# Scan, first chunk, attention side and x1 stage of a fused attention and FFN block

## The chip, the cores and the metric

The kernel runs on one core of one Trainium2 chip. The metric is device time in microseconds of one execution. "The span" is the time between the first and the last instruction that the profile of one execution shows.

## What is computed

1024 tokens of width 512 are normalised to `xn`. From it come two branches, and the output is `x + s * silu(f)`.

```python
xn = layernorm(x)
# attention-like branch: 4-bit weights, looked up in a table and scaled by blocks of 64, each with a rank-16 term
attn = (lin(xn, Wq) + lin(xn, Wk) + lin(xn, Wv)) / 3
x1 = xn + lin(attn, Wo)
h = silu(lin(x1, Wg)) * lin(x1, Wu)                  # 512 -> 1792
s = x1 + lin(h, Wd)                                  # 1792 -> 512
# FFN branch, weights from f32 pairs (w, mean)
W = mean + average(abs(w - mean)) * sign(w - mean)   # one average over a whole 1792x512 matrix, three matrices
f = lin(silu(lin(xn, W1)) * lin(xn, W3), W2)
out = x + s * silu(f)
```

## The kernel before

All products use f32r operands split in a high and a low part: three matmuls (high x high, high x low, low x high) per product. 1792 is cut in 14 chunks of 128; chunks 0 to 13 belong to the FFN branch, 14 to 27 to the second half of the 4-bit branch. A chunk's gate projection for one half of the tokens (512 columns) is 4 x 3 = 12 matmuls; so are its up projection and the other half. `h = silu(gate) * up` is made by ScalarE and VectorE and split. A down stage (D0 to D9) multiplies the `h` of two or three chunks with their down weights into 8 output tiles; three PSUM banks `down_ps` take turns, ScalarE evicts each (`y_evict`), and from D1 on GpSimd's queue adds the evicted tile to `y` or `y2` by an accumulating DMA (`y_add`, four slots `y_part`).

**Front.** The three averages need every element of `w - mean`. Chunks 0 to 3 are held on the chip as 12 units (gate 0 to 3, up 4 to 7, down 8 to 11; 128x512 pairs). Chunks 4 to 13 are only scanned: 15 tiles of 128x1024 pairs, 5 for each matrix, which go through a buffer of 4 slots (`scan`, L346). VectorE subtracts (L863), ScalarE writes the signs as int8 (L556), stores them to memory (L561) and sums the absolute values (L558). Units 0 to 3 are subtracted by VectorE, 4 to 11 by GpSimd (L506), and summed by ScalarE (L574). `take_coeff(m)` reduces the partial sums (L906), TensorE adds them over the partitions (`total`, L1235), VectorE scales them (L909). Then a unit is made (`unit_make`, L916), its high part is written by ScalarE (L584) and its low part by VectorE (L924), and TensorE projects. All gate projections of chunks 0 to 3 come first, then all up projections, then D0. `total(UP)` stands on TensorE's queue behind `project(3, GATE, 0)`, `total(DOWN)` behind `project(2, UP, 1)`.

**Middle.** From D0 on the order is written out in `STAGES`: D0, 4, 5, 6, D1, 7, 8, 9, D2, 10, 11, 12, D3, 13, X, D4, T, 14 and so on. A numbered stage (`phase`) projects that chunk. Each engine goes through the stages in this order. VectorE makes the weights of the next FFN chunk from `base` and the stored `sign` (`ffn_make`, L932), both loaded by SP (`load_ffn`). Beside this runs the attention side: the product of Wo with the sum of Wq, Wk and Wv is folded to one 512x512 matrix `MT`. It takes 40 steps (`attn_step`: a ramp on ScalarE, L668, and a min-add on VectorE, L1002; five steps for half a row block, codes by `load_attn`), some more for sums and splits, and 24 small groups of matmuls into the one bank `side_ps` (`ATTN_SIDE` lists behind which projection or tile each stands: per row block of 4, `lora_qkv`, `lora_o` and four `fold`s, L1303). Each needs the bank emptied by VectorE (L1015, L1019, L1032), the folds also the low parts (L1023, L1025). `ATTN_COUNT` lists the steps per stage.

**x1, D4, T.** Stage X computes x1 = MT times xn in 8 tiles (L1356), which replace xn in `xT` (high ScalarE L822, low VectorE L1182). D4 is the last down stage of the FFN branch, T the rank-16 part of gate and up (L1369, high L831, low L1195). In between run the first steps for the 4-bit chunks (`nf4_step`, ramp L688, VectorE L1041, scale L1047, and the rank term `lora_add` L948). On GpSimd's queue: `y_add` for D1 to D3, then four additions that sum the parts of x1 to `y2` (L524), then `y_add` for D4. On SP's queue, in this order around D2: ..., load_attn(5), a wait for the end of D2, A_down (L436), load_ffn(11), load_ffn(12), load_attn(6), load_ffn(13), load_attn(7), ...; `B_gu` (the rank terms' second factor) is loaded in two halves into one buffer (L448, L453), scaled (L742), split (L749, L1108), and the first use of its gate half and of T is the 13th matmul of a projection of chunk 14 (L1258).

## Time and profile before

| | |
|---|---|
| time of 3 runs, us | 665.79 (662.33 to 666.79) |
| the profiled execution, us | 665.82 |
| its span, us | 664.0 |
| TensorE matmul busy | 558.6 us, 84% |
| VectorE busy | 463.6 us, 70% |
| ScalarE busy | 376.4 us, 57% |
| GpSimd busy | 113.3 us, 17% |
| moved by DMA | 76.72 MB |

The profile is of one execution. "Busy" is the time in which an engine executes; the shares are averages over stages of very different kinds, so they are to be read stage by stage. The granted clock is TensorE's, as a share of 2.4 GHz. A row of idle time names what ended it.

### The profile page before, as it was taken

The page shows a single profiled execution, that of the slowest core. Times are in us where ns is not written, and L with a number is a line of the kernel's source. Part 1 is how long each engine was busy: PE and PEld are TensorE (multiplying, and loading weights), DVE is VectorE, ACT ScalarE, POOL GpSimd, SP SyncE. Part 2 cuts the span into 40 slices and gives each one's busy share as a digit, 9 for nine tenths or more (in the row PEclk, how much of TensorE's full clock was granted, in tenths as well). Part 3 has the DMA queues.
Part 4 walks back from the last instruction along what each step waited for, and adds up shares of the span by engine and source line. Part 5 has one row for each costly group of instructions (what it writes and reads, how often), then busy time and mean ns, then how long its engine had stood idle before and what let it go on. Part 6 is the DMA issues. An engine that isn't in the chain of part 4 may idle for free.

```text
span 664.0 us, 6488 instructions
## 1 busy us (share of the span) xinstructions
PE 558.6 (84%) x2304; PEld 447.9 (67%) x2304; DVE 463.6 (70%) x512; ACT 376.4 (57%) x494; POOL 113.3 (17%) x110
## 2 busy tenths in 40 slices
PE   1168688999999759888698479989899998999997
PEld 1155466888888647667586257767677886887886
DVE  6770548688887628772419947888888888988436
ACT  3866576657744634542237265587559667676310
POOL 0021323001300310022000930012004002101491
PEclk9778888999999888998988778979999999999999
DMA  9979531131820472045201362247217325623903
GB/s 339 401 272 391 209 117 63 61 126 41 178 84 0 80 216 84 0 105 107 52 1 33 74 122 60 61 91 155 59 33 138 80 57 122 123 59 80 221 1 126
DMA packets 37951, 76.72 MB, mean 116 GB/s; under 512 B 3872, under 2 KB 11936, under 8 KB 37920
## 3 DMA queue, kind: packets, MB, share of 16 engines
q1 hardware_dynamic: 24624, 57.57, 27.4%
q0 software_dynamic: 9216, 16.78, 14.2%
q10 hardware_dynamic: 4080, 1.97, 1.0%
q8 instruction: 18, 0.29, 0.2%
q14 instruction: 13, 0.11, 0.1%
HBM read 55.46 MB, written 4.06 MB: 90 GB/s over the span
## 4 chain that ended last, share of the span: by engine, by line
PE 45%; DVE 23%; ACT 14%; issue 10%; DMA 4%; POOL 2%; SPq 0%; ACTq 0%; DVEq 0%
PE down_ps L1278 17%; PE up_ps L1250 13%; PE gate_ps L1250 10%; DVE acc L1041 9%; ACT ramp L688 5%; POOL y L524 2%; PE side_ps L1303 2%; ACT sign_st L556 2%; PE down_ps L1356 2%; DVE up_ps L958 1%; DVE scan L863 1%; DMA sign<-sign_kept 1%; DMA scan<-in_mean 1%; ACT y_part L635 1%; DMA y<-y_part 1%
## 5 line engine op out<-in xcount | busy, mean ns | idle before, releaser
L1278 PE MATMUL down_ps<-h,dn 128*128 128x512 f32 x672 | 169.7, 410 | 18.9 <-ACT y_part L635 18.9
L1250 PE MATMUL up_ps<-xT,gu 128*128 128x512 f32 x672 | 167.4, 401 | 11.2 <-DVE h L963 11.1
L1250 PE MATMUL gate_ps<-xT,gu 128*128 128x512 f32 x672 | 168.0, 402 | 10.3 <-ACT silu_gate L617 7.2
L1278 PEld LDWEIGHTS down_ps<-h,dn 128*128 128x128 f32 x672 | 132.4, 199 | 52.2 <-ACT y_part L635 23.4
L1250 PEld LDWEIGHTS up_ps<-xT,gu 128*128 128x128 f32 x672 | 130.6, 195 | 41.6 <-issue 9.7
L1250 PEld LDWEIGHTS gate_ps<-xT,gu 128*128 128x128 f32 x672 | 129.8, 194 | 41.2 <-issue 9.3
L1041 DVE SCALAR_TENSOR_TENSOR acc<-ramp,acc 128x1536 f32<-128x1536 f32 x56 | 102.4, 1829 | 30.4 <-ACT ramp L688 29.7
L514 POOL DMA_DIRECT2D y<-y_part x64 | 55.5, 933 | 383.3 <-ACT y_part L635 383.2
L688 ACT ACTIVATE ramp<-codes,ramp_bias 128x1536 f32<-128x1536 uint8 x70 | 109.8, 1574 | 1.2 <-DVE acc L1041 1.2
L622 ACT ACTIVATE h<-up_ps 128x512 fp32r<-128x512 f32 x56 | 33.5, 597 | 112.7 <-DVE up_ps L955 60.0
L635 ACT ACTIVATE y_part<-down_ps 128x512 f32<-128x512 f32 x64 | 37.5, 596 | 45.5 <-PE down_ps L1278 33.1
L1002 DVE SCALAR_TENSOR_TENSOR attn_acc<-attn_ramp,attn_acc 128x1024 f32<-128x1024 f32 x40 | 49.4, 1235 | 14.7 <-ACT attn_ramp L668 14.6
L963 DVE TENSOR_TENSOR h<-up_ps,h 128x512 fp32r<-128x512 f32 x56 | 38.5, 688 | 16.6 <-ACT h L622 16.4
L617 ACT ACTIVATE silu_gate<-gate_ps 128x512 f32<-128x512 f32 x56 | 32.9, 587 | 22.9 <-PE gate_ps L1250 12.7
L668 ACT ACTIVATE attn_ramp<-attn_codes,ramp_bias 128x1024 f32<-128x1024 uint8 x40 | 45.8, 1144 | 0.0
L1041 DVE SCALAR_TENSOR_TENSOR acc<-ramp,codes 128x1536 f32<-128x1536 f32 x14 | 24.5, 1752 | 15.2 <-ACT ramp L688 15.1
L1303 PE MATMUL side_ps<-w_o,w_qkv 128*128 128x512 f32 x48 | 15.5, 434 | 22.1 <-DVE MT_acc L1032 15.5
L932 DVE SCALAR_TENSOR_TENSOR base<-sign,coeff,base 128x512 f32<-128x512 int8 x30 | 23.7, 844 | 12.9 <-DMA sign<-sign_kept 12.9
L955 DVE TENSOR_TENSOR up_ps<-silu_gate,up_ps 128x512 f32<-128x512 f32 x28 | 19.4, 692 | 17.5 <-PE up_ps L1250 17.5
L958 DVE SCALAR_TENSOR_TENSOR up_ps<-up_ps,silu_gate 128x512 f32<-128x512 f32 x28 | 19.4, 694 | 12.8 <-PE up_ps L1258 12.8
L1303 PEld LDWEIGHTS side_ps<-w_o,w_qkv 128*128 128x128 f32 x48 | 9.1, 201 | 26.4 <-issue 17.0
L1047 DVE SCALAR_TENSOR_TENSOR acc<-acc,scale 128x1536 f32<-128x1536 f32 x14 | 24.6, 1758 | 0.5
(155 smaller groups left out, 508.0 us busy)
## 6 DMA issues: line engine op xcount, KB each, us to landing
y<-y_part POOLq DMA_DIRECT2D x64, 256.0 KB, 3.6
...
scan<-in_w SPq DMA_DIRECT2D x15, 512.0 KB, 7.4
scan<-in_mean SPq DMA_DIRECT2D x15, 512.0 KB, 8.3
...
```

What stands on the lines that cost most here:

```text
L514: pool.dma_start((y if g < FFN_GROUPS else y2)[:, hq, sl], y_part[:, q % Y_SLOTS, :], accum_op=ALU.add).then_inc(y_added[q % Y_SLOTS], 16)
L617: nc.scalar.activation(silu_buf(k, th), gate_ps[th][:, :], ACT.Silu, scale=1.0 if k < B0 else UNIT_STEP).then_inc(silu_done, 1)
L622: nc.scalar.activation(h_part(k, HI, th), up_ps[th][:, :], ACT.Copy).then_inc(h_hi, 1)
L635: nc.scalar.activation(place, down_ps[n % 3][:, :], ACT.Copy, scale=1.0 if g < FFN_GROUPS else UNIT_STEP).then_inc(y_out, 1)
L668: nc.scalar.activation(attn_ramp[:, s % 2, :, :], attn_codes[:, a % 2, :, :], ACT.Relu, bias=ramp_bias[:, 0, j:j + 1], scale=slope).then_i ...
L688: nc.scalar.activation(ramp[:, s % 2, :], codes[:, k % 2, :], ACT.Relu, bias=ramp_bias[:, 1, j:j + 1], scale=slope).then_inc(nf4_ramped, 1)
L963: nc.vector.tensor_tensor(h_part(k, LO, th), up_ps[th][:, :], h_part(k, HI, th).bitcast(f32), ALU.subtract).then_inc(h_lo, 1)
L1002: nc.vector.scalar_tensor_tensor(attn_acc[:, a % 2, :, :], attn_ramp[:, s % 2, :, :], NF4_RAMPS[j][2], attn_acc[:, a % 2, :, :], ALU.min, ...
L1041: nc.vector.scalar_tensor_tensor(acc[k % 2][:, :], ramp[:, s % 2, :], UNIT_RAMPS[j][2], codes[:, k % 2, :] if j == 0 else acc[k % 2][:, :] ...
L1250: last = nc.tensor.matmul(ps[:, :], w[:, w_part, hc * P:(hc + 1) * P], xT[:, x_part, hc, th * HALF:(th + 1) * HALF], start=(hc == 0 and w_ ...
L1278: last = nc.tensor.matmul(down_ps[n % 3][:, :], dn[:, k % DN_SLOTS, w_part, hq * P:(hq + 1) * P], h_part(k, h_p, th), start=(k == ks[0] an ...
L1303: last = nc.tensor.matmul(side_ps[:, :], w_qkv[:, a_part, hc * P:(hc + 1) * P], w_o[:, b_part, :], start=(a_part == b_part == HI), stop=(a ...
```

## The change

1. *Scan.* The buffer becomes two: 5 slots for w and 3 for mean; mean is loaded first, and its slot is free when the subtraction is done, w's when sign and sum are. 4 slots for signs instead of 2. Subtractions of tiles 7, 9, 11 and 13 move from VectorE to GpSimd, the absolute sums of tiles 3, 4, 6, 8, 9, 11, 13 and 14 from ScalarE to VectorE (`tensor_reduce`).
2. *First chunk.* The gate projection of chunk 0 is computed as mean part (24 matmuls, `early_mean`) plus coefficient times sign part (16 matmuls, `early_signs`; signs need no low part), which VectorE adds (`early_sum`). Unit 0 is never made. Chunks 1 and 3 use `gate_ps` for their up projection, so that the wait for `h_lo` is for two chunks back. The orders of ScalarE and VectorE are rewritten.
3. *Attention side.* New `ATTN_COUNT` and `ATTN_SIDE`; MT's high and low parts are made inside stage 13; loads of SP are reordered.
4. *x1, D4, T.* Two 4-bit steps come ahead of x1's evictions; `y2` is filled by a DMA of the high part (SP) and four accumulating DMAs of the low part (GpSimd's queue), behind D4's `y_add`; T's parts come before the step of that stage; in down stages of two chunks the steps stand behind tiles 0, 3, 5, 7.

```diff
-SCAN_SLOTS = 4
-SIGN_SLOTS = 2
+SCAN_W, SCAN_MEAN = 5, 3
+SIGN_SLOTS = 4
+POOL_SCAN = [7, 9, 11, 13]
+DVE_SUMS = [3, 4, 6, 8, 9, 11, 13, 14]
...
-ATTN_COUNT = {"D0": (0, 3), 4: (0, 3), 5: (0, 2), 6: (0, 4), "D1": (0, 4), 7: (0, 3), 8: (0, 2), 9: (0, 4),
-              "D2": (0, 4), 10: (0, 3), 11: (0, 2), 12: (0, 4), "D3": (0, 8), 13: (0, 5)}
+ATTN_COUNT = {"D0": (0, 3), 4: (0, 3), 5: (0, 2), 6: (0, 4), "D1": (0, 4), 7: (0, 3), 8: (0, 3), 9: (0, 5),
+              "D2": (0, 4), 10: (0, 3), 11: (0, 3), 12: (0, 4), "D3": (0, 7), 13: (3, 0)}
...
-ATTN_SIDE = [(4, 3), ("D1", 0), (7, 0), (7, 2), (8, 0), (8, 2),
-             (8, 3), (9, 2), ("D2", 2), ("D2", 5), ("D2", 7), (10, 1),
-             (10, 2), (11, 0), (12, 2), ("D3", 0), ("D3", 1), ("D3", 3),
-             ("D3", 4), ("D3", 5), (13, 0), (13, 1), (13, 2), (13, 3)]
+ATTN_SIDE = [(4, 3), ("D1", 0), (7, 0), (7, 2), (7, 3), (8, 1),
+             (8, 2), (8, 3), ("D2", 1), ("D2", 3), ("D2", 5), ("D2", 7),
+             (10, 0), (10, 1), (11, 3), (12, 1), (12, 2), ("D3", 0),
+             ("D3", 1), ("D3", 3), ("D3", 6), ("D3", 7), (13, 0), (13, 1)]
...
             def load_scan(k):
...
-                if k >= SCAN_SLOTS:
-                    sp.wait_ge(scan_abs, k - SCAN_SLOTS + 1)
+                if k >= SCAN_MEAN:
+                    diff_wait(sp, k - SCAN_MEAN)
+                sp.dma_start(scan_mean[:, k % SCAN_MEAN, :].rearrange("p (c n) -> p c n", c=2),
...
+                if k >= SCAN_W:
+                    sp.wait_ge(scan_sign, k - SCAN_W + 1)
+                    sum_wait(sp, k - SCAN_W)
+                sp.dma_start(scan_w[:, k % SCAN_W, :].rearrange("p (c n) -> p c n", c=2),
...
             load_attn(5)
+            load_ffn(11)
+            load_attn(6)
+            load_ffn(12)
             sp.wait_ge(down_done, 3 * TT)
             sp.dma_start(A_down_raw[0:ROWS3, 0:INTER], A_down_in).then_inc(A_down_loaded, 16)
-            load_ffn(11)
-            load_ffn(12)
-            load_attn(6)
+            load_attn(7)
             load_ffn(13)
-            load_attn(7)
...
-            load_scale(B0 + 1)
-            load_codes(B0 + 2)
+            sp.wait_ge(x1_lo, TT)
+            sp.wait_ge(MT_lo, HC)
+            sp.dma_start(y2[:, :, :], xT[:, HI, :, :].bitcast(f32)).then_inc(y2_copied, 16)
             sp.wait_ge(B_gu_hi, 1)
             sp.wait_ge(B_gu_lo, 1)
             sp.dma_start(B_gu_raw[0:ROWS3, 0:INTER], B_gu_in[:, UP, :]).then_inc(B_gu_loaded, 16)
+            load_scale(B0 + 1)
+            load_codes(B0 + 2)
...
-            for u in range(FIRST, UNITS):
-                unit_subtract(u)
+            for kind in (UP, DOWN):
+                for n in range(SCAN_TILES):
+                    if scan_on_pool(SCAN_TILES * kind + n):
+                        scan_subtract(SCAN_TILES * kind + n)
+                    if n > 0:
+                        unit_subtract(FIRST * kind + n - 1)
             attn_tables()
-            for g in range(1, FFN_GROUPS - 1):
+            for g in range(1, FFN_GROUPS):
                 y_add(g)
-            pool.wait_ge(x1_lo, TT)
+            pool.wait_ge(y2_copied, 16)
             for hc in range(HC):
-                nc.gpsimd.tensor_tensor(y2[:, hc, :], xT[:, HI, hc, :].bitcast(f32), xT[:, LO, hc, :].bitcast(f32),
-                                        ALU.add).then_inc(y2_ready, 1)
-            y_add(FFN_GROUPS - 1)
-            pool.wait_ge(y2_ready, HC)
+                pool.dma_start(y2[:, hc, :], xT[:, LO, hc, :].bitcast(f32), accum_op=ALU.add).then_inc(y2_ready, 16)
+            pool.wait_ge(y2_ready, 16 * HC)
...
+            def early_high():
+                act.wait_ge(unit_loaded[0], 32)
+                nc.scalar.activation(gu_weight(0, GATE)[:, HI, :], unit_base(0), ACT.Copy).then_inc(gu_hi, 1)
+
+            def early_sign():
+                act.wait_ge(unit_diff_dve, 1)
+                nc.scalar.activation(sign_T, unit_raw(0), ACT.Sign).then_inc(unit_sign, 1)
...
+            def scan_sum(k):
+                kind, n = k // SCAN_TILES, k % SCAN_TILES
+                diff_wait(dve, k)
+                nc.vector.tensor_reduce(abs_sums[:, SUMS * kind + n:SUMS * kind + n + 1], scan_w[:, k % SCAN_W, :],
+                                        axis=AX.X, op=ALU.add, apply_absolute_value=True).then_inc(scan_abs_dve, 1)
...
+            def early_sum(th):
+                dve.wait_ge(gate_done, th + 1)
+                nc.vector.tensor_scalar(silu_buf(0, th), up_ps[th][:, :], coeff[:, GATE:GATE + 1], None, ALU.mult
+                                        ).then_inc(early_part, 1)
+                dve.wait_ge(early_part, th + 1)
+                nc.vector.tensor_tensor(early_ps[th][:, :], early_ps[th][:, :], silu_buf(0, th), ALU.add
+                                        ).then_inc(early_gate, 1)
...
+            early_mean(0)
+            early_mean(1)
+            early_signs(0)
             total(GATE)
-            for c in range(FIRST):
+            early_signs(1)
+            for c in range(1, FIRST):
```

VectorE's new order in the front (sums moved to it are bold): x_low 0 to 3, early_low, unit_subtract(0), x_low 4 to 7, subtract 2, unit 1, subtract 3, unit 2, **sum 3**, subtract 4, unit 3, **sum 4**, take_coeff(GATE), unit_make(1), early_sum(0), unit_low(1), subtract 5, unit_make(2), early_sum(1), unit_low(2), unit_make(3), subtract 6, unit_low(3), **sum 6**, subtract 8, **sum 8**, **sum 9**, take_coeff(UP), unit_make 4, 5, low 4, make 6, low 5, make 7, low 6, subtract 10, low 7, **sum 11**, h_make(0, 0), subtract 12, h_low(0, 0), h_make(0, 1), h_low(0, 1), **sum 13**, h_make(1, 0), subtract 14, h_low(1, 0), **sum 14**, h_make(1, 1), h_low(1, 1), take_coeff(DOWN).

## Rows read from the trace of the kernel before

**Rows 1.** The page of the profile, its first line.

```profile
span 664.0 us, 6488 instructions
```

**Rows 2.** Busy time by stage: window, length, engines, granted clock, DMA share, GB/s.

```profile
38.40:109.60 71.20, 55.23 (x197) 42.60 (x198) 37.48 (x49) 44.40 (x82) 15.34 (x14) 0.86 0.61 216
109.60:217.80 108.20, 108.20 (x478) 89.25 (x476) 88.75 (x106) 67.85 (x92) 13.62 (x13) 1.00 0.28 75
217.80:331.70 113.90, 87.81 (x353) 69.84 (x352) 64.81 (x84) 47.77 (x66) 13.25 (x16) 0.91 0.39 94
331.70:399.20 67.50, 50.30 (x183) 38.71 (x184) 43.17 (x31) 34.68 (x39) 20.62 (x12) 0.82 0.28 56
399.20:660.20 261.00, 251.13 (x1064) 201.84 (x1062) 201.83 (x183) 158.60 (x177) 48.40 (x48) 0.98 0.41 91
```

**Rows 3.** Timeline of TensorE, front: start us, us, engine, line, count, idle before.

```profile
38.40 7.32 PE L1250 MATMUL gate_ps<-xT,gu 128*128 128x512 f32 x24 [2.73 <-DVE gu L924]
...
73.84 5.61 PE L1250 MATMUL up_ps<-xT,gu 128*128 128x512 f32 x24
...
109.48 16.48 PE L1278 MATMUL down_ps<-h,dn 128*128 128x512 f32 x72
```

**Rows 4.** Timeline of ScalarE, front: an Abs and the issue of a store.

```profile
28.80 1.04 ACT L558 ACTIVATE scan<-scan 128x1024 f32<-128x1024 f32 x1
28.92 0.37 ACTq L561 DMA_DIRECT2D sign_kept<-sign_st  x1
```

**Rows 5.** Timeline of VectorE, front: subtraction, partial sum, coefficients, last low parts.

```profile
23.39 0.68 DVE L899 TENSOR_TENSOR xT<-side_ps,xT 128x512 fp32r<-128x512 f32 x1
...
27.45 1.23 DVE L863 TENSOR_TENSOR scan<-scan 128x1024 f32<-128x1024 f32 x1
...
34.80 0.16 DVE L906 TENSOR_REDUCE abs_part<-abs_sums 128x1 f32<-128x9 f32 x1 [5.53 <-ACT junk L574]
...
66.62 0.16 DVE L909 TENSOR_SCALAR coeff<-side_ps 128x1 f32<-128x1 f32 x1 [7.17 <-PE side_ps L1235]
...
98.60 0.16 DVE L909 TENSOR_SCALAR coeff<-side_ps 128x1 f32<-128x1 f32 x1 [3.21 <-PE side_ps L1235]
...
104.70 1.28 DVE L924 TENSOR_TENSOR dn<-unit_lr,dn 128x512 fp32r<-128x512 f32 x2
```

**Rows 6.** GpSimd's subtractions of unit_lr: min/median/max ns.

```profile
L506 POOL TENSOR_TENSOR unit_lr<-unit_lr x2: 1277/2358/3439, 65.9 to 69.7; 128x512 f32<-128x512 f32 x2
```

**Rows 7.** DMA of the first 75 us in 40 slices, and an issue's time to landing.

```profile
GB/s 3 322 375 364 371 409 402 406 406 398 405 404 398 405 403 401 399 398 404 399 401 400 189 0 74 196 383 373 365 398 406 403 382 400 409 405 84 0 0 70
...
scan<-in_mean SPq DMA_DIRECT2D x15, 512.0 KB, 8.3
```

**Rows 8.** Who waited for whom, 200 to 420 us: total, times, longest.

```profile
PE side_ps L1303 <- DVE MT_acc L1032: 15.5, 4, 9.4
DVE base L932 <- DMA sign<-sign_kept: 12.9, 1, 12.9
...
PE side_ps L1303 <- DVE w_o L1025: 6.7, 3, 3.7
...
PE down_ps L1356 <- DVE MT L1204: 4.0, 1, 4.0
```

**Rows 9.** Timeline of SP's queue: the load of sign for chunk 11.

```profile
236.11 0.42 SPq L365 DMA_DIRECT2D sign<-sign_kept  x1
```

**Rows 10.** Who waited for whom, 200 to 420 us: TensorE in D4.

```profile
PE down_ps L1278 <- ACT y_part L635: 11.9, 2, 9.5
```

**Rows 11.** Timeline of GpSimd: the sum of x1's parts.

```profile
366.29 13.68 POOL L524 TENSOR_TENSOR y<-xT 128x1024 f32<-128x1024 f32 x4 [52.87 <-DVE xT L1182]
```

**Rows 12.** Timeline of VectorE and ScalarE: B_gu's low part and high part.

```profile
363.46 2.02 DVE L1108 TENSOR_TENSOR B_gu<-B_gu_raw,B_gu 32x1792 fp32r<-32x1792 f32 x1
...
332.28 1.70 ACT L749 ACTIVATE B_gu<-B_gu_raw 96x1792 fp32r<-96x1792 f32 x1
```

**Rows 13.** DMA queues, 360 to 400 us: packets, MB, share of 16 engines.

```profile
q0 software_dynamic: 1152, 2.10, 29.2%
```

More of the change, by code:

```diff
@@ L1117, in _ @@
                 x_low(t)
+            early_low()
             unit_subtract(0)
@@ L1200, in _ @@
                         A_down_low()
-                    if stage == 13:
-                        for c in range(HC):
-                            dve.wait_ge(MT_hi, c + 1)
-                            nc.vector.tensor_tensor(MT[:, LO, c, :], MT_acc[:, c, :], MT[:, HI, c, :].bitcast(f32),
-                                                    ALU.subtract).then_inc(MT_lo, 1)
                 else:
```

279 lines of the change are left out of this document (195 added, 84 removed).

## Prediction

> **What bounds the kernel now.** I read the busy time by stages first, because shares of the whole span mix stages with different limits. The span is 664.0 us [rows 1]. From 109.6 to 217.8 us TensorE is busy the whole 108.20 us with 478 matmuls at granted clock 1.00: 108.20/478 = 0.226 us per matmul of 512 columns. That is the pace of a stage with nothing to gain. With it the other stages can be priced: time lost = length minus matmuls x 0.226. From 38.4 to 109.6: 71.2 - 197 x 0.226 = 26.7 us lost. From 217.8 to 331.7: 113.9 - 353 x 0.226 = 34.1. From 331.7 to 399.2: 67.5 - 183 x 0.226 = 26.1. From 399.2 to 660.2: 261.0 - 1064 x 0.226 = 20.5 [rows 2]. With the 38.4 us before the first projection these are all that can be won; TensorE's own work is the bound everywhere else. A part of each loss is the clock: it is 0.86, 0.91 and 0.82 in the first three of these stages, so a pause is paid twice, by itself and by matmuls at 1.2 instead of 2.4 GHz after it.
>
> **Front: scan, first chunk.** Before, TensorE starts its projections at 38.40, the up projections at 73.84 and D0 at 109.48 [rows 3]. What it waits for are three coefficients on VectorE: the first partial sum comes at 34.80 and its coefficient 0.9 later, the other two coefficients at 66.62 and 98.60 [rows 5]. Each comes after the last of the absolute sums. ScalarE pays for a tile an Abs of 1.04 and a sign of the same shape [rows 4], some 2.1 us.
>
> *Gate coefficient.* Tiles 3 and 4 now have their sums on VectorE. A reduction of 128x1024 isn't in the trace. Nearest: the subtraction of the same shape, 1.23 us [rows 5]; bounds 0.68 (half the width, the x_low row) and 2.46 (twice the subtraction); I take 1.15. ScalarE does not save a full Abs: the store of the signs waits for the sign and then takes 0.37 on its queue, which the Abs used to cover [rows 4]; so a tile without Abs costs about 1.5, saving 0.65, not 1.1. ScalarE also gets early_high and early_sign (0.5 each). Stepping through the two orders from the last x_low (start 23.39, moved 0.6 later by early_low): VectorE does subtract 2, unit 1, subtract 3, unit 2, sum 3, subtract 4, unit 3, sum 4, ending at 32.2; ScalarE ends its fourth unit sum at 31.8. The partial sum comes at 32.2 instead of 34.80, the coefficient at 33.1.
>
> *First chunk.* early_mean is 24 matmuls in place of the 24 of chunk 0, early_signs 16 more (16 x 0.226 = 3.6 us of extra TensorE work). 32 of these run from 21.7 to about 30.7, in today's pause, and hide. The last 8 come while VectorE makes unit 1. Chunk 1 starts at about 36.6, with chunk 0 done: as if the old 38.40 were 31.2 (36.6 less 24 x 0.226). The added vector work is early_sum (2 x 1.3) and early_low (0.6), that taken away one unit_make.
>
> *Up coefficient.* Here is the big term. Before, TensorE reached total(UP) only after project(3, GATE, 0), which waited for a silu that stood behind full scan tiles on ScalarE. Now the scan of tiles 5 to 9 has three Abs less and two subtractions on GpSimd. I step SP too: the mean buffer has 3 slots and is freed by the subtraction, so tiles 5 to 9 are issued at about 26, 28, 30, 37 and 42 us. The data flow at 400 GB/s when the queue is full, and a tile lands 8.3 us after issue in such a queue [rows 7]; tile 9 lands at 47. GpSimd's subtraction of 128x1024 isn't in the trace; half the width takes 1.28 alone and 3.44 at worst beside VectorE [rows 6], so 2.6 to 6.9; I take 2.6 with 1 us of waiting. Then tile 9's difference is there at 49 to 50, its sum at 51, the last unit sum at 51.3, the coefficient at 52.5. Up projections start at 56 to 57 instead of 73.84.
>
> *Down coefficient.* The load now bounds it. x, 15 tile pairs of 1.05 MB and 12 unit pairs of 0.52 MB are 24.1 MB, 60 us at 400 GB/s; 3 us start, some 3 for the stored signs and 4 to 6 of pauses (mean 13 waits for subtraction 10, which follows the up coefficient's unit work) make 70 to 72. Behind it stand subtraction 14, sum 14, two h steps and the total: coefficient at about 77 to 79 instead of 98.60. TensorE pauses 2 to 4 us at total(DOWN). From coefficient to the third unit's low part it took 98.60 to 105.98 = 7.4 us [rows 5]; I keep 7.4, so D0 starts at 86.5 (82 to 92) instead of 109.48. **Term 1: -23 us** (-17 to -27).
>
> On GpSimd the Trainium skill (SBUF — State Buffer, "Who interferes with whom") says that a VectorE instruction with two SBUF inputs contends with a GpSimd instruction that reads SBUF, and that one blocks the other whole, while tensor_reduce never contends. The trace's 3.44 against 1.28 us agrees with the first half [rows 6]. By that rule up to 4 x 2.6 = 10.4 us of VectorE work would be pushed back, and term 1 could shrink to about -15.
>
> **Attention side, 217.8 to 331.7.** TensorE pauses before the fold matmuls for 15.5 us (4 times, longest 9.4) behind MT_acc and 6.7 us (3 times) behind w_o, and 4.0 before the x1 stage behind MT's low part [rows 8]; with the slow clock after each that is the stage's 34.1.
>
> The 9.4: VectorE sat 12.9 us for sign of chunk 11 [rows 8], whose load was issued at 236.11, right behind A_down's, which waits for the end of D2 [rows 9]. Moving load_ffn(11), load_attn(6) and load_ffn(12) ahead of that wait frees it: load_ffn(11) needs only chunk 9's split. A_down, load_attn(7) and load_ffn(13) then follow at D2's end and are needed in stage 11 or later, one stage of 48 matmuls (10.9 us) away, against at most 8.3 us of landing [rows 7]. Worth 9.4 + 1.6 of clock = 11.
>
> The rest: attention steps come 1 to 2 steps earlier from stage 8 on and the folds sit later relative to them: a fold of the second row block follows its low parts by a stage part, and the last four sit at D3 6, 7 and 13 0, 1 with MT's splits inside stage 13 in place of behind it. That removes the 6.7, the other 6.1 and the 4.0, with about 6 us of clock: 23. Against it stands VectorE. Over 109.6 to 217.8 it was busy 88.75 of 108.20 with 25 attention steps and, beside them, two down stages and six phases [rows 2]. Stages 7 to 12 (D2 among them) now hold 25 steps, six phases and one down stage in 91 us of TensorE time (400 matmuls): 88.75 less some 5 for the down stage's own work is 84, or 92%, and stage 9 alone has five steps where four were the most. So I expect short waits of 4 to 5 us in all. **Term 2: -29 us** (-17 to -33).
>
> **x1, D4 and T, 331.7 to 399.2.** GpSimd's y2 sum takes 13.68 us ahead of D4's additions [rows 11]; TensorE waits 9.5 us behind y_part because of it, and 2.4 more there [rows 10]. Now D4's additions go first; y2 is filled by a DMA and four accumulating DMAs, needed only in D5. By stepping: VectorE ends x1's low part 3 only 0.5 earlier (the steps still lie between), but lora_add comes some 4 us earlier, since one step and the scaling no longer stand ahead and GpSimd's reads no longer run beside it; with the 9.5 and 2.4 gone and some 3 of slow clock, D4 ends about 14 us earlier, at 371 to 373. Then B_gu's second half is late next: its load is behind the 2.1 MB copy on SP's queue. The nearest price is the accumulating queue, 2.10 MB in 29.2% of 40 us = 11.7 us [rows 13]; D4's own additions are as much again at the same time. So copy and additions fill 361 to about 380, B_gu lands at 378 to 382, its scaling and high part (1.70 each) and its low part (2.02) [rows 12] end at 386, and T's low part at 386 to 387; TensorE stands some 7 us at the first matmul with T. That point was 399.2, the end of the stage [rows 2]. **Term 3: -13 us** (-2 to -18). load_scale(15) and load_codes(16), now behind B_gu, are wanted only after T: nothing.
>
> **Late part.** D5's steps are spread over its short tiles; of the 20.5 us lost there [rows 2] I take 3 (0 to 6). **Term 4: -3.**
>
> **Sum.** 664.0 - 23 - 29 - 13 - 3 = 596.0 us of span. The profiled execution took 665.82 us, 1.8 over its span and equal to the median of 665.79: **597.8, say 598 us**.
>
> **Rivals.** (a) *GpSimd holds back the scan*: its subtractions take up to 6.9 us and block VectorE; tiles 7, 9 and 13 each cost 3 to 4 more on the path: term 1 becomes -13, 608 us. For it: 3.44 us; against: sums on VectorE have one input. 14 in 100. (b) *The copy delays B_gu by its full price*: if D4's additions, the copy and the accumulations run one after another at the accumulating queue's rate, 3 x 11.7 = 35 us from 361, then B_gu's 2 + 5.4, T comes at 403 and term 3 is +4: 615 us. 10 in 100. (c) *VectorE becomes the bound of the attention side*, stages 9 to 12 run 8 to 12 us over: 609 us. 12 in 100. (d) *It goes better*: no residual waits, B_gu in time: 583 or less. 8 in 100. (e) *Slower than before*: denser matmuls are held at 1.2 GHz. Each costs 0.226 more; to eat 68 us, 301 more than now would have to run so, one in eight. Against it the 478 matmuls in a row at clock 1.00 [rows 2]. 2 in 100. The forecast itself, 585 to 606 with its terms' errors, has 54.
>
> The range 583 to 612 takes in (a), (c) and the forecast. About 1% is what a measurement can tell from no change. Faster by over 1% (under 659) is every case but (e): 97 in 100; same 1; slower 2.
>
> **What would show it.** D0's first matmul at about 86; coefficients at 33, 52 and 78; tensor_reduce near 1.15 us and GpSimd's subtraction near 2.6; no load of sign waiting on VectorE's path at D2; no pause over 2 us before folds; D4 over by 373 and a pause of about 7 us before the first T matmul. The forecast is wrong if D0 starts after 95, if VectorE's waits turn into TensorE's in stages 9 to 12, or if B_gu lands after 390.

## The result and the profile after

The changed kernel takes 614.35 us (median of 4 runs, 612.87 to 614.86), the kernel before in the same comparison 666.29 us (4 runs, 662.33 to 667.77). The ratio is 0.9225, 95% interval 0.9182 to 0.9269: 7.7% faster. Predicted were 598 us and a range of 583 to 612. The sign was right; the gain was 52 us where 68 were forecast, and the time lies 2.4 us above the range. One execution of the kernel before (830.77 us) and one of a kernel below (779.53 us) showed a granted clock near 0.66, and no figure here uses them.

The profiled execution has a span of 612.2 us. Cut at the same four points as the sum of the prediction (gate projections, D0, x1, first matmul behind T), the stages are the following. Columns as in [rows 2]: window, length, busy us and count of TensorE, its weight loads, VectorE, ScalarE, GpSimd, then granted clock, DMA share and GB/s.

```profile
36.35:91.20 54.85, 45.74 (x174) 35.69 (x173) 44.95 (x50) 36.03 (x65) 25.14 (x19) 0.87 0.82 293
91.20:285.99 194.79, 189.20 (x830) 154.69 (x828) 154.24 (x191) 117.32 (x161) 27.49 (x28) 1.00 0.41 102
285.99:345.96 59.97, 46.17 (x184) 35.76 (x184) 32.44 (x30) 33.29 (x38) 10.45 (x12) 0.90 0.51 116
345.96:608.40 262.44, 251.36 (x1064) 202.61 (x1062) 204.93 (x183) 158.91 (x178) 48.38 (x48) 0.98 0.42 95
```

The boundaries of the kernel before are 109.48 [rows 3], 331.68 and 399.22 in its timeline (331.70 and 399.20 in [rows 2]), and 660.2 us. So the terms measured are:

| term | before | after | measured | predicted |
|---|---|---|---|---|
| 1: up to D0 | 109.48 | 91.20 | -18.3 | -23 (-17 to -27) |
| 2: D0 to x1 | 222.20 | 194.79 | -27.4 | -29 (-17 to -33) |
| 3: x1 to behind T | 67.54 | 59.97 | -7.6 | -13 (-2 to -18) |
| 4: late part | 261.0 | 262.4 | +1.5 | -3 (0 to -6) |
| sum of the span | 664.0 | 612.2 | -51.8 | -68 |

All four terms fell short, by 4.7, 1.6, 5.4 and 4.5 us. Three of them are within their own bounds; the fourth is outside, and all four missed in one direction. The second row shows what term 2 brought: 194.79 us for the stretch in which 188 us of matmuls at full speed stand (830 at 0.226), at a clock of 1.00 where it was 0.95 before over the same stretch. The profiles of six kernels of this study that leave this stretch as it is have 196.5 to 196.6 us here and not 194.8, so term 2 is -25.7 to -27.4 us.

**Front after.** VectorE's timeline (start us, us, engine, line, operation, shapes, count, idle time before it and what ended it):

```profile
33.37 0.16 DVE L1012 TENSOR_SCALAR coeff<-side_ps 128x1 f32<-128x1 f32 x1 [0.48 <-PE side_ps L1391]
...
40.45 2.47 DVE L1027 TENSOR_TENSOR gu<-unit_st,gu 128x512 fp32r<-128x512 f32 x1
42.84 1.77 DVE L1019 SCALAR_TENSOR_TENSOR unit_st<-unit_st,coeff 128x512 f32<-128x512 f32 x1
44.54 1.21 DVE L960 TENSOR_TENSOR scan_w<-scan_w,scan_mean 128x1024 f32<-128x1024 f32 x1
...
53.47 1.22 DVE L966 TENSOR_REDUCE abs_sums<-scan_w 128x1 f32<-128x1024 f32 x1 [2.52 <-POOL scan_w L572]
...
56.40 0.16 DVE L1012 TENSOR_SCALAR coeff<-side_ps 128x1 f32<-128x1 f32 x1 [0.68 <-PE side_ps L1391]
...
66.54 1.21 DVE L960 TENSOR_TENSOR scan_w<-scan_w,scan_mean 128x1024 f32<-128x1024 f32 x1
...
73.12 0.69 DVE L1058 TENSOR_TENSOR up_ps<-silu_gate,up_ps 128x512 f32<-128x512 f32 x1
...
83.44 0.16 DVE L1012 TENSOR_SCALAR coeff<-side_ps 128x1 f32<-128x1 f32 x1 [0.68 <-PE side_ps L1391]
```

and GpSimd's of the same time:

```profile
39.97 2.40 POOL L572 TENSOR_TENSOR scan_w<-scan_w,scan_mean 128x1024 f32<-128x1024 f32 x1 [1.38 <-DMA scan_w<-in_w]
42.32 1.75 POOL L567 TENSOR_TENSOR unit_st<-unit_st 128x512 f32<-128x512 f32 x1
...
51.07 2.36 POOL L572 TENSOR_TENSOR scan_w<-scan_w,scan_mean 128x1024 f32<-128x1024 f32 x1 [4.18 <-DMA scan_w<-in_w]
53.41 1.26 POOL L567 TENSOR_TENSOR unit_st<-unit_st 128x512 f32<-128x512 f32 x1
...
73.07 2.41 POOL L572 TENSOR_TENSOR scan_w<-scan_w,scan_mean 128x1024 f32<-128x1024 f32 x1 [7.00 <-DMA scan_w<-in_w]
```

Two unit instructions of VectorE, which take 0.68 and 0.75 us elsewhere in the same view, take 2.47 and 1.77 here. Each ends 0.5 us after a GpSimd subtraction does: 40.45 + 2.47 = 42.92, and GpSimd's ends at 42.37; 42.84 + 1.77 = 44.61, and GpSimd's at 44.07. Five more such rows stand between 37 and 66 us, of 1.76 to 2.43 us, and each of them ends 0.5 to 0.6 us behind GpSimd's too. Two kinds of VectorE's instructions run beside GpSimd without being stretched: the reduction at 53.47 has its usual 1.22 us beside GpSimd's instruction of 53.41, and the h step at 73.12, one of whose inputs lies in PSUM, takes 0.69 beside that of 73.07. The three coefficients come at 33.37, 56.40 and 83.44, against 35.7, 66.62 and 98.60 before (the first is the 34.80 of [rows 5] and 0.9).

**x1, D4 and T after.** Who waited for whom, 286 to 348 us (total us, times, longest), and then the DMA issues of 290 to 380 us (count, KB of one, median us from issue to landing):

```profile
ACT y_part L716 <- DMA y<-y_part: 12.5, 4, 5.3
...
PE gate_ps L1420 <- DVE T L1337: 7.3, 1, 7.3
...
PE down_ps L1440 <- ACT y_part L716: 4.0, 2, 3.8
```

```profile
y<-y_part POOLq DMA_DIRECT2D x8, 256.0 KB, 11.2
y<-xT SPq DMA_DIRECT2D x1, 2048.0 KB, 11.0
y<-xT POOLq DMA_DIRECT2D x4, 512.0 KB, 8.8
B_gu_raw<-in_B_gu SPq DMA_DIRECT2D x1, 672.0 KB, 15.8
```

TensorE's 9.5 us wait of [rows 10] has become 3.8. ScalarE stands 12.5 us for y_part's slots, as long as in the kernel before, from 331.7 to 400 us:

```profile
ACT y_part L635 <- DMA y<-y_part: 12.4, 3, 10.2
```

Then GpSimd's sum held the additions back, which landed 4.9 us after their issue; now they are issued in time and take 11.2 us to land.

### The profile page after: what moved, and what is told of

It reads as the page before. It is cut to its first block, busy times and chain, and to the rows that moved or that the text cites. A ratio compares the mean times of both kernels' runs of the same rounds, so it can differ in the third digit from the quotient of the medians.

```text
span 612.2 us, 6544 instructions
## 1 busy us (share of the span) xinstructions
PE 549.9 (90%) x2320; PEld 442.9 (72%) x2320; DVE 467.6 (76%) x519; ACT 367.3 (60%) x478; POOL 112.3 (18%) x114
## 4 chain that ended last, share of the span: by engine, by line
PE 40%; DVE 25%; issue 13%; ACT 11%; DMA 7%; SPq 1%; POOL 1%; ACTq 0%; DVEq 0%
PE down_ps L1440 13%; PE up_ps L1412 10%; PE gate_ps L1412 10%; DVE acc L1144 9%; ACT ramp L769 7%; DMA y<-y_part 4%; DMA scan_w<-in_w 2%; DVE up_ps L1061 2%; PE side_ps L1465 2%; DVE scan_w L960 2%; DVE h L1066 1%; PE down_ps L1518 1%; DVE attn_acc L1105 1%; ACT y_part L716 1%; DMA unit_end<-in_mean 1%
## 5 line engine op out<-in xcount | busy, mean ns | idle before, releaser
L1412 PE MATMUL gate_ps<-xT,gu 128*128 128x512 f32 x696 | 174.3, 404 | 1.2 <-ACT silu_gate L698 0.5
L1440 PE MATMUL down_ps<-h,dn 128*128 128x512 f32 x672 | 161.2, 395 | 11.3 <-ACT y_part L716 11.3
L1412 PEld LDWEIGHTS gate_ps<-xT,gu 128*128 128x128 f32 x696 | 136.0, 196 | 32.5 <-DVE gu L1027 1.5
L1440 PEld LDWEIGHTS down_ps<-h,dn 128*128 128x128 f32 x672 | 126.5, 190 | 42.3 <-ACT y_part L716 14.8
L1412 PE MATMUL up_ps<-xT,gu 128*128 128x512 f32 x624 | 152.0, 395 | 4.4 <-DVE h L1066 3.8
L1412 PEld LDWEIGHTS up_ps<-xT,gu 128*128 128x128 f32 x624 | 118.6, 191 | 31.4 <-DVE h L1066 4.5
L1144 DVE SCALAR_TENSOR_TENSOR acc<-ramp,acc 128x1536 f32<-128x1536 f32 x56 | 98.3, 1756 | 43.0 <-ACT ramp L769 42.4
L703 ACT ACTIVATE h<-up_ps 128x512 fp32r<-128x512 f32 x52 | 31.1, 598 | 100.7 <-DVE up_ps L1061 51.8
L1066 DVE TENSOR_TENSOR h<-up_ps,h 128x512 fp32r<-128x512 f32 x52 | 35.7, 686 | 15.2 <-ACT h L703 15.1
L698 ACT ACTIVATE silu_gate<-gate_ps 128x512 f32<-128x512 f32 x54 | 31.7, 588 | 23.0 <-PE gate_ps L1412 15.8
L1058 DVE TENSOR_TENSOR up_ps<-silu_gate,up_ps 128x512 f32<-128x512 f32 x24 | 16.6, 691 | 11.8 <-PE up_ps L1412 11.8
L1040 DVE TENSOR_TENSOR gu<-acc,gu 128x1024 fp32r<-128x1024 f32 x14 | 17.0, 1217 | 5.5 <-ACT gu L675 5.5
L1135 DVE TENSOR_TENSOR MT_acc<-MT_acc,side_ps 128x512 f32<-128x512 f32 x16 | 10.9, 681 | 12.7 <-PE side_ps L1465 12.7
```

What stands on the lines that cost most here:

```text
L698: nc.scalar.activation(silu_buf(k, th), ps[:, :], ACT.Silu, scale=1.0 if k < B0 else UNIT_STEP).then_inc(silu_done, 1)
L703: nc.scalar.activation(h_part(k, HI, th), up_bank(k, th)[:, :], ACT.Copy).then_inc(h_hi, 1)
L1066: nc.vector.tensor_tensor(h_part(k, LO, th), up_bank(k, th)[:, :], h_part(k, HI, th).bitcast(f32), ALU.subtract).then_inc(h_lo, 1)
L1144: nc.vector.scalar_tensor_tensor(acc[k % 2][:, :], ramp[:, s % 2, :], UNIT_RAMPS[j][2], codes[:, k % 2, :] if j == 0 else acc[k % 2][:, :] ...
L1412: last = nc.tensor.matmul(ps[:, :], w[:, w_part, hc * P:(hc + 1) * P], xT[:, x_part, hc, th * HALF:(th + 1) * HALF], start=(hc == 0 and w_ ...
L1440: last = nc.tensor.matmul(down_ps[n % 3][:, :], dn[:, k % DN_SLOTS, w_part, hq * P:(hq + 1) * P], h_part(k, h_p, th), start=(k == ks[0] an ...
```

## The experiments

Each kernel is the changed kernel with the edit shown. Ratios are to the kernel before on the same chip, with their 95% intervals; for the changed kernel itself it is 0.9225 [0.9182, 0.9269] and 614.35 us. Intervals overlap where kernels differ by 3 us or less, so such differences are read from boundaries in the profiles too.

### Front: GpSimd's subtractions

```
-POOL_SCAN = [7, 9, 11, 13]
+POOL_SCAN = []
```

> The changed kernel with tiles 7, 9, 11 and 13 of the scan subtracted by VectorE again (everything else of the change stays). Theory (GpSimd's reads slow VectorE's instructions with two SBUF inputs, and so cost the front about as much as they save): the instructions of unit_make and unit_low between 37 and 47 us and between 59 and 67 us fall from 1.8 and 2.4 us to about 0.75 and 0.7 where only a tile subtraction lay beside them; VectorE does 4 x 1.15 us more; D0 starts at 88 to 92 instead of 91.2, the whole within 0.5% of the changed kernel (609 to 617). Rival (the offload is a plain gain, the loss lies elsewhere): D0 4 to 5 us later, 617 to 620.

Measured: 611.71 us, 0.9203 [0.917, 0.9236]. VectorE's timeline:

```profile
33.25 0.16 DVE L1012 TENSOR_SCALAR coeff<-side_ps 128x1 f32<-128x1 f32 x1 [0.68 <-PE side_ps L1391]
...
40.32 0.68 DVE L1027 TENSOR_TENSOR gu<-unit_st,gu 128x512 fp32r<-128x512 f32 x1
...
54.30 0.16 DVE L1012 TENSOR_SCALAR coeff<-side_ps 128x1 f32<-128x1 f32 x1 [0.48 <-PE side_ps L1391]
...
78.58 0.16 DVE L1012 TENSOR_SCALAR coeff<-side_ps 128x1 f32<-128x1 f32 x1 [0.48 <-PE side_ps L1391]
```

The low part at 40 us is back at 0.68, and the coefficients are 2.1 and 4.9 us earlier, although VectorE does four subtractions more. Its groups of instructions by line, 34 to 90 us, give the account. The subtractions cost 14.0 us for ten instead of 7.3 for six: 6.7 us had been moved to GpSimd. The seven low parts of line L1027 and the eight products of unit_st, line L1019, cost 5.9 + 7.0 us instead of 10.5 + 9.1: 6.7 us had come back as blocking. What is left of blocking in this kernel (1.78 us at 37 and at 60 us, 2.32 at 41) stands beside the unit subtractions, which GpSimd made before the change as well. So the move took nothing off VectorE, while a difference made by GpSimd takes 2.4 us and not 1.2, and VectorE waited 2.52 us for that of tile 9 (the row at 53.47 above). D0 starts at 86.02 instead of 91.20, and at 87.41 in a later kernel with the same front. The prediction had said 86.5, but for a kernel in which GpSimd does subtract.

Only about half of that arrives at the end (2.6 us of the medians):

```profile
86.02:284.23 198.21, 192.58 (x829) 157.12 (x829) 154.63 (x191) 117.41 (x161) 27.49 (x28) 0.98 0.41 101
```

The stretch from D0 to x1 is 198.21 us instead of 194.79 with the same 4.8 us of waits for folds; the granted clock is 0.98 instead of 1.00. D0's 72 matmuls take 18.25 us behind a pause of 1.89, instead of 16.48 without one (granted clock 0.91 instead of 1.00), and 12 matmuls behind the fold pause at 243 us take 4.12 instead of 2.90 (0.67 over 243.6 to 248.7, where the changed kernel has 1.00). So 1.2 GHz was granted for a part of each. The second of these isn't the edit's: behind the same pause of 2.8 us the clock stayed at 1.00 in four profiles of this study and fell in six others that leave this stretch as it is. With the late copy (below) the same edit moves D0 from 90.95 to 87.41 and x1 from 287.43 to 284.01, and the median by 3.7 us, so there it arrives in full.

### Front: one more slot for the means

```
-SCAN_W, SCAN_MEAN = 5, 3
+SCAN_W, SCAN_MEAN = 4, 4
```

> The changed kernel with 4 slots for w and 4 for mean instead of 5 and 3 (the same memory). Theory (the loads of tiles 9 and 13 are late because the mean slot is freed by a subtraction of three tiles back, which stands behind coefficient work on VectorE): tile 9 is issued at about 40 instead of 45.8, tile 13 at 55 to 58 instead of 67.8, coefficients at 52 to 54 and 76 to 79, D0 at 84 to 87 instead of 91.2, so 607 to 610. Rival (the data rate bounds the front, 24 MB at 400 GB/s): issues earlier, landings the same, D0 within 1 us, 613 to 615.

Measured: 612.43 us, 0.9217 [0.9183, 0.9252]; coefficients at 33.68, 55.67, 82.52, D0 at 89.96. The mean of tile 9 is issued at 38.64 instead of 45.78 and that of tile 13 at 55.22 instead of 67.77, that is 7 and 12.5 us earlier. The coefficients moved by 0.7 and 0.9. So the issue of the loads was not what held them; 1.9 us of time can't be told from nothing.

### Front: subtraction 10 ahead of the up coefficient

```
             scan_sum(9)
+            scan_subtract(10)
             take_coeff(UP)
...
             unit_low(6)
-            scan_subtract(10)
             unit_low(7)
```

> The subtraction of scan tile 10 goes ahead of the up coefficient on VectorE; before, it stood behind that coefficient's unit work and ended at 67.8 us. Theory (down coefficient late because mean 13 waits for subtraction 10): mean 13 is issued 8 to 11 us earlier, at 57 to 60; the down coefficient comes at 77 to 80 instead of 83.4, D0 at 85 to 88 instead of 91.2; the up coefficient 1.2 to 2.4 us later (57.6 to 59). Of the 4 to 5 us, 1 to 4 reach the end: 611 to 613. Rival (the stored signs, the units and the total amount of data bound it): the down coefficient stays within 1.5 us of 83.4, time 614 to 616.

Measured: 614.75 us, 0.9223 [0.9179, 0.9266]: the rival. VectorE's two coefficients:

```profile
58.36 0.16 DVE L1012 TENSOR_SCALAR coeff<-side_ps 128x1 f32<-128x1 f32 x1 [0.68 <-PE side_ps L1391]
...
83.83 0.16 DVE L1012 TENSOR_SCALAR coeff<-side_ps 128x1 f32<-128x1 f32 x1 [0.56 <-PE side_ps L1391]
```

The mean of tile 13 is issued at 57.64 instead of 67.77, 10 us earlier, as the theory had it, and the down coefficient still comes at 83.83. My theory of what delays it fell. Put side by side over the kernels of this study, the distance from the up to the down coefficient is 83.44 - 56.40 = 27.0 us in the changed kernel, 24.3 without GpSimd's part, 26.9 with four mean slots, 25.5 here and, in the three kernels with both cures below, 24.2, 25.7 and 26.2. The two shortest issued tile 13's mean at 57.48 and 63.10, the kernel with 26.9 at 55.22 and the one with 26.2 at 53.73, so the distance doesn't follow the loads. It does scatter: 24.3 and 25.7 are of the same front, and six kernels with the changed kernel's front have 26.2 to 27.1. The rows between the two coefficients show VectorE working through its fixed order, with a wait of only 0.34 us for a load: low parts, subtractions and sums in between, and each h step behind the up projections, which start behind the up coefficient; the last sum (79.48 to 80.69 in the changed kernel) is followed by two h steps of chunk 1, and then comes the total. That the order is the bound is read from these rows. No kernel changed the order of the h steps, so it is not shown.

### Attention side: the order of the loads

```
-            load_ffn(11)
-            load_attn(6)
-            load_ffn(12)
             sp.wait_ge(down_done, 3 * TT)
             sp.dma_start(A_down_raw[0:ROWS3, 0:INTER], A_down_in)...
+            load_ffn(11)
+            load_attn(6)
+            load_ffn(12)
```

> Only the order of SyncE's loads is undone: A_down's load with its wait for the end of D2 stands again ahead of chunk 11's codes and signs, attention step 6 and chunk 12. Theory (term 2: 11 of the 29 us came from here): the time returns to 614.4 + 11 = about 625 us (622 to 628), VectorE waits some 9 to 12 us for the sign of chunk 11 during D2, and TensorE stands 7 to 9 us in one piece before a fold in stage 11 or 12. Rival (the moved steps and folds alone bring the 27 us and VectorE had slack): the wait on VectorE returns but TensorE loses under 3 us: 614 to 617.

Measured: 624.28 us, 0.9366 [0.9324, 0.9408], 9.9 us slower. TensorE's timeline and who waited for whom, 190 to 300 us:

```profile
226.12 0.79 PE L1452 MATMUL side_ps<-A_qkv,B_qkv_hi 128*128 128x512 f32 x1 [8.37 <-DVE MT_acc L1135]
```

```profile
ACT attn_acc L743 <- DMA attn_codes<-in_codes_attn: 13.9, 1, 13.9
```

The pause of 8.37 us is back, and x1 comes 297.15 - 90.52 = 206.6 us after D0 instead of 194.8: 11.8 us in this stretch, or 10.1 against the 196.5 of most kernels. The size is that of the step. The one who waits for a late load is ScalarE, for the codes of an attention step, and no longer VectorE for the sign of chunk 11 as in [rows 8].

### Attention side: steps, folds and MT's splits

```
-              ... 8: (0, 3), 9: (0, 5),
-              ... 11: (0, 3), 12: (0, 4), "D3": (0, 7), 13: (3, 0)}
+              ... 8: (0, 2), 9: (0, 4),
+              ... 11: (0, 2), 12: (0, 4), "D3": (0, 8), 13: (0, 5)}
 ATTN_SIDE = [... the list of the kernel before ...]
 MT_high(), MT_low(c): behind phase(13), as before
```

> The tables of attention steps and folds are those of the kernel before, and the splits of MT follow stage 13 as they did; the new order of SyncE's loads stays. Theory (term 2 in two parts: 10 us from the loads, as their undoing showed with 624.3 us, the rest of the 27.4 from steps and folds): 614.4 + 15 to 18 = 629 to 632 us; TensorE waits behind MT_acc and w_o before folds and some 4 us before the x1 stage. Rival (with the load no longer late, VectorE catches up by itself and the old folds cost little): 617 to 622.

Measured: 630.21 us, 0.9457 [0.9418, 0.9496], 15.9 us slower. TensorE's timeline, the longest pauses:

```profile
203.13 1.65 PE L1460 MATMUL side_ps<-w_o,w_qkv 128*128 128x512 f32 x3 [3.70 <-DVE w_o L1127]
...
272.16 1.62 PE L1460 MATMUL side_ps<-w_o,w_qkv 128*128 128x512 f32 x3 [3.57 <-DVE MT_acc L1134]
...
303.69 10.12 PE L1513 MATMUL down_ps<-xT,MT 128*128 128x512 f32 x36 [3.19 <-DVE MT L1198]
```

The waits behind w_o (6.7 us, 3 times, as in [rows 8]), three behind MT_acc and one behind MT return; x1 comes 212.7 us after D0, 17.9 more. With the 11.8 of the loads this is 29.7, and both together had brought 27.4. Both kernels run slow behind a fold pause of 2.8 and 2.6 us, as those with 196.5 do; against these the halves are 10.1 and 16.2, together 26.3, where term 2 is -25.7. The two halves of term 2 are shown and add up: 11 predicted for the loads, 18 for steps and folds.

### x1 to T: the copy to y2, later

```
-            sp.wait_ge(x1_lo, TT)
-            sp.wait_ge(MT_lo, HC)
-            sp.dma_start(y2[:, :, :], xT[:, HI, :, :].bitcast(f32)).then_inc(y2_copied, 16)
             sp.wait_ge(B_gu_hi, 1)
...
             load_codes(B0 + 2)
+            sp.wait_ge(x1_lo, TT)
+            sp.wait_ge(MT_lo, HC)
+            sp.wait_ge(y_out, TT * FFN_GROUPS)
+            sp.dma_start(y2[:, :, :], xT[:, HI, :, :].bitcast(f32)).then_inc(y2_copied, 16)
```

> The changed kernel with the copy of x1's high part to y2 moved on SP's queue behind B_gu's second half, scale and codes, and held back until D4's tiles are evicted. Theory (copy and D4's additions share the DMA engines, so additions land in 11.2 us instead of 3.6 and B_gu in 15.8 instead of 5): additions land in under 5 us, ScalarE's waits for y_part (12.5 us) and TensorE's (3.8 us) go, B_gu lands at about 322, the wait of 7.3 us for T falls under 1 us; with slow clock 12 to 15 us less: 600 to 603. Rival (ScalarE and VectorE's steps bound this stretch, the waits only lie in their slack): the same stretch is at most 4 us shorter: 610 to 613.

Measured: 607.23 us, 0.9137 [0.9098, 0.9175], 7.1 us less than the changed kernel. DMA issues, 290 to 380 us, and TensorE's first matmul with T:

```profile
y<-y_part POOLq DMA_DIRECT2D x8, 256.0 KB, 8.6
...
B_gu_raw<-in_B_gu SPq DMA_DIRECT2D x1, 672.0 KB, 5.5
```

```profile
338.93 0.79 PE L1421 MATMUL gate_ps<-T,B_gu 96*128 96x512 f32 x1 [2.65 <-DVE T L1338]
```

From x1 to this matmul it is 338.93 - 287.43 = 51.5 us, in the changed kernel 345.37 - 285.99 = 59.4. So the copy at its old place cost 7.9 us there, and nearly all of it reaches the end. The 12 to 15 us that I expected were too much: the additions still take 8.6 us to land.

### x1 to T: B_gu ahead of the copy

```
             sp.wait_ge(B_gu_hi, 1)
             sp.wait_ge(B_gu_lo, 1)
             sp.dma_start(B_gu_raw[0:ROWS3, 0:INTER], B_gu_in[:, UP, :]).then_inc(B_gu_loaded, 16)
+            (the copy to y2 and its two waits, moved here)
```

> The copy to y2 goes behind the load of B_gu's second half on SyncE's queue, and so still runs beside D4's additions; before, it went ahead of it. Theory (two separate costs: B_gu late behind the copy, and D4's additions slowed beside it; only the first goes): B_gu lands in 5 to 8 us, but the additions stay at 9 to 11 us, TensorE's waits in D4 stay at 2 to 4 us and T waits 4 to 7 us, because ScalarE, which scales B_gu, stands behind y_part's slots: 611 to 614 us. Rival (B_gu's late landing is the whole of the missing 5.5 us): as with the copy behind D4, 607 to 608.

Measured: 613.1 us, 0.9196 [0.9158, 0.9234]: no difference that can be told. DMA issues, then ScalarE's and TensorE's timelines:

```profile
y<-y_part POOLq DMA_DIRECT2D x8, 256.0 KB, 10.1
...
B_gu_raw<-in_B_gu SPq DMA_DIRECT2D x1, 672.0 KB, 5.6
```

```profile
333.43 0.60 ACT L716 ACTIVATE y_part<-down_ps 128x512 f32<-128x512 f32 x1 [7.57 <-DMA y<-y_part]
...
340.24 1.68 ACT L834 ACTIVATE B_gu_raw<-B_gu_raw 96x1792 f32<-96x1792 f32 x1
```

B_gu's half lands 5.6 us after its issue at 318.31, by 324, and ScalarE scales it only at 340.24, because it stood 7.57 us for a slot of y_part. TensorE waits 10.4 us at T. From x1 to the first T matmul it is 56.55 us, against 57.8 to 59.9 in the seven kernels with both the copy and B_gu at the changed kernel's places and 51.3 to 51.5 in those with the late copy. This tells the two causes apart: B_gu's late landing, which the prediction named, is worth 1 to 3 us at most of the 8; what decides is that D4's additions land late beside the copy, and that the in-order ScalarE has B_gu behind them. When TensorE ends D4 doesn't decide either: here, with four mean slots and with the old pace of D5 it ended 37.6 to 37.9 us after x1, 5 us earlier than in the changed kernel, and then waited 10.4, 12.2 and 11.7 us at T.

### x1 to T: y2's sum by GpSimd

```
-            pool.wait_ge(y2_copied, 16)
+            pool.wait_ge(x1_lo, TT)
+            pool.wait_ge(MT_lo, HC)
             for hc in range(HC):
-                pool.dma_start(y2[:, hc, :], xT[:, LO, hc, :].bitcast(f32), accum_op=ALU.add)...
+                nc.gpsimd.tensor_tensor(y2[:, hc, :], xT[:, HI, hc, :]..., xT[:, LO, hc, :]..., ALU.add)...
```

The copy is gone too; the sum stands behind D4's additions, where it stood ahead of them in the kernel before.

> y2 is made by GpSimd in four additions as before the change, but behind D4's additions: no copy by DMA and no accumulating DMA for it; D4's additions of the queue go first. Theory (the copy and the accumulations share the DMA engines with D4's additions and B_gu, and that cost the missing 5.5 us of term 3): D4's additions land in 4 to 6 us instead of 11.2, B_gu's second half in under 6 instead of 15.8, TensorE waits under 3 us at the first T matmul and 0 to 1 us in D4, T starts 6 to 9 us earlier after the x1 stage (51 to 53 us instead of 59.4); 606 to 608 us, as with the late copy, if D5's additions aren't late. Rival (D4's additions are slow by themselves, because 8 of them come in 12 us): they stay at 8 us or more, T waits 4 us or more: 610 to 614.

Measured: 613.51 us, 0.9193 [0.9126, 0.926]. The stage did what the theory said: D4's additions land in 6.5 us, B_gu in 5.2, TensorE waits 3.28 at T, and x1 to T is 51.7 us. But the time is that of the changed kernel. GpSimd's, VectorE's and TensorE's timelines show where the 8 us went:

```profile
331.80 15.74 POOL L592 TENSOR_TENSOR y<-xT 128x1024 f32<-128x1024 f32 x4
```

```profile
341.45 3.83 DVE L1149 SCALAR_TENSOR_TENSOR acc<-acc,scale 128x1536 f32<-128x1536 f32 x1
345.20 3.95 DVE L1143 SCALAR_TENSOR_TENSOR acc<-ramp,codes 128x1536 f32<-128x1536 f32 x1
```

```profile
365.46 4.76 PE L1411 MATMUL up_ps<-xT,gu 128*128 128x512 f32 x12 [5.17 <-DVE h L1065]
```

Two instructions of 1.76 us take 3.83 and 3.95 beside GpSimd, VectorE is 5 us late, and TensorE waits 5.17 at 365 us and 4.92 at 423 for h, where it waited 0.85 and 2.80 in the changed kernel. This is the same cost as in the front, and it is the case for the copy by DMA.

### Late part: D5's pace

```
-                    elif len(GROUPS[g]) == 3:
+                    elif len(GROUPS[g]) == 3 or g >= FFN_GROUPS:
```

> The changed kernel with the steps of D5 placed on ScalarE as before (behind tiles 0, 2, 3, 4), D4 stays as changed. Theory (the new places save little there): TensorE's pauses and slow matmuls in D5 go from 4.4 to about 6 us, time +1 to +2 us. Rival (the new places are the reason for the loss of 1.5 us after T): -1 to -3 us.

Measured: 614.19 us, 0.924 [0.9209, 0.9272]: nothing. TensorE's pauses in D5 are 2.74, 0.16 and 0.32 us, in the changed kernel 2.68, 0.37 and 1.33. The shorter pauses are paid for behind the first of them, where 12 matmuls take 4.85 us at a granted clock of 0.64, while in the changed kernel the clock stays up.

### The cures together

Three kernels have both cures, POOL_SCAN = [] and the late copy. The first has subtraction 10 ahead of the up coefficient as well, the second nothing else, the third SCAN_W, SCAN_MEAN = 4, 4.

> Three edits together: no scan subtraction on GpSimd, tile 10's subtraction ahead of the up coefficient, and the copy to y2 behind D4's 40 sums. Theory (the terms are apart: front and T stage add up): 607.2 (copy alone) less 2.6 (no GpSimd subtraction alone) less 0 to 2 = 603 to 605; D0 at 83 to 86. Rival (the end of the x1 stage is set by something else, so that a front gain is lost at the T matmuls, where B_gu's load already waits for queued loads): 606 to 608.

> Two edits: no scan subtraction on GpSimd, and the copy to y2 behind D4's 40 sums. Tile 10's subtraction stays behind the up coefficient. Theory (that early subtraction put VectorE 2 to 3 us behind at the up coefficient and brought nothing): 607.2 - 2.6 = 604.6, less 0 to 1: 603.5 to 605; D0 at 86. Rival (the front's gain is given back on the way to x1, by the slow clock): 605.5 to 607.

> As the kernel with two edits (no scan subtraction on GpSimd, late copy), with 4 slots for the scan's means and 4 for its weights instead of 3 and 5. Theory (with GpSimd's subtractions gone, the loads are issued early enough with either split): within 1 us of the other, D0 at 84 to 87. Rival (a mean slot more lets tiles 9 and 13 be loaded some 6 us earlier, and the down coefficient follows the load): D0 at 81 to 83, and 1.5 to 3 us less.

| kernel | us | ratio, interval | D0 | x1 | first T matmul |
|---|---|---|---|---|---|
| with subtraction 10 first | 605.81 | 0.9082 [0.9038, 0.9125] | 89.82 | 286.35 | 337.60 |
| the two cures alone | 603.58 | 0.9064 [0.9032, 0.9096] | 87.41 | 284.01 | 335.52 |
| and 4 mean slots | 602.28 | 0.9038 [0.9004, 0.9072] | 88.88 | 283.70 | 335.13 |

The two cures add up: 614.35 - 7.1 - 2.6 = 604.6 against 603.58 measured. Subtraction 10 ahead of the coefficient has D0 2.4 us later and is no help: the up coefficient comes at 58.20 instead of 54.23. Four mean slots can't be told from three: D0 didn't come at 81 to 83 as the rival for that kernel had it. The mean of tile 13 was issued at 53.73 there, ahead of the up coefficient at 54.84, and the down coefficient still came 26.2 us behind the up coefficient. The best kernel is 2.0% below the changed one (602.28/614.35).

## Why the prediction missed, step by step

**Term 1, front: mechanism right, one size wrong.** Right were the gate coefficient (33.1 said, 33.37 measured), chunk 1's start (36.6, 36.35), the reduction of 128x1024 (1.15, 1.21 us) and GpSimd's subtraction (2.6, 2.4). Wrong was the step "I take 2.6 with 1 us of waiting" for GpSimd's part: it priced the subtractions alone and took VectorE's unit work at its usual 0.68 and 0.75. In its place: each of the seven VectorE instructions with two SBUF inputs that started beside one of GpSimd's ended 0.5 us behind it, 1.0 to 1.8 us longer than alone. Subtraction 6 stands behind three of them, and so tile 9 was issued at 45.78 instead of 42. The up coefficient came at 56.40 instead of 52.5, the up projections at 62.00 instead of 56 to 57 and the down coefficient at 83.44 instead of 77 to 79; from there to D0 it was 7.8 us, 7.4 said. Taking the four subtractions off GpSimd gave 54.30, 78.58 and D0 at 86.02; 54.23, 79.96 and 87.41 in the second kernel with that front. The Trainium skill's rule (SBUF — State Buffer, "Who interferes with whom"), that one instruction blocks the other whole and a tensor_reduce never contends, stood in the prediction beside the sum, with "about -15" as its result. The rows bear the rule out in kind, by the ends that fall 0.5 us behind GpSimd's and the reduction's unchanged 1.21; the measured -18.3 lies between its -15 and my -23, and not all of GpSimd's subtractions met a two-input instruction: the one at 51.07 fell into a wait of VectorE. It is rival (a), at half its price.

A second step was wrong and cost nothing: "The load now bounds it" for the down coefficient. Four kernels issued tile 13's mean 10 to 14 us earlier, and the down coefficient stayed 24 to 27 us behind the up coefficient. That 78.58 lies in the predicted 77 to 79 when GpSimd's subtractions are gone is luck: the path that gave the number isn't the one that bound.

**Term 2, attention side: right.** -27.4 against -29 (-25.7 against the 196.5 of most kernels), and its two parts, by their undoing, 10 to 12 and 16 to 18 against 11 and 18. The waits left were said to be 4 to 5 us: they are 1.07, 0.93, 2.79 and 0.69 = 5.5. VectorE was busy 39.62 of the 45 us between 200 and 245, 88%. The longest of these waits, 2.79, is for it, but they stayed far from the 8 to 12 us of rival (c).

**Term 3, x1 to T: the wrong wait.** D4 was to end 40 us after x1 and ended 42.7 after it (TensorE goes on to T's matmuls at 328.71, and x1 started at 285.99); before it was 54.9. T's low part was to be there 54 to 55 us after x1, and the first T matmul started 59.4 after it. That the pause at T was 7.30 where the prediction said "some 7" is luck: D4 and T's low part were both later than said, and in three other kernels of this study that end D4 earlier the pause was 10.4 to 12.2. The cause was misnamed: B_gu landed at 315.62 + 15.8 = 331.4, or 45.4 after x1, in time with the 46 to 50 that the prediction allowed; but ScalarE came to it only at 339.14, behind four waits for y_part's slots. The prediction counted the copy against B_gu alone and D4's additions at no delay, although the sentence before had them "at the same time". What the runs showed: behind the copy an addition takes 11.2 us to land, 8.6 with the copy late and 6.5 without it. Moving B_gu ahead changed the time by nothing that can be told and the stage by 1 to 3 us, moving the copy behind D4 gave 7.1 us. Rival (b) had the right resource, but too high a price, and put it on B_gu.

**Term 4, late part: no gain.** -3 was taken without a row that showed the wait as one of D5's pace. In this kernel the new pace was worth nothing (614.19 us with the old one). The largest pause of the late part, 2.80 at 423.59, is for an h low part that stands behind three instructions of 128x1536 on VectorE, as it did before with 2.48 at 475.96. Behind it TensorE ran slower:

```profile
423.59 5.49 PE L1412 MATMUL up_ps<-xT,gu 128*128 128x512 f32 x12 [2.80 <-DVE h L1066]
```

5.49 us for 12 matmuls at a granted clock of 0.50, where they took 3.02 at 1.00 before: that is 2.5 us and more than the +1.5 of the term. The same 12 matmuls take 4.35 to 5.49 in the other profiled kernels of this study, so it isn't this execution alone. Why the clock is lower there than before, behind a pause of nearly the same length, stays open.

**The range.** Its upper bound, 612, was 2.4 us too low. It took in rivals (a) and (c) one at a time, each with the other terms at their forecast; what came was a part of (a), a delay of D4's additions that no rival had, and a late part without gain, together. With either cure alone the time is inside the range (611.71 and 607.23).
